# A graph convolution with nearest neighbours: two-piece float32r gathers, a sigmoid adjacency, and thresholds and widening on GpSimd

## What is computed

```python
emb = jnp.einsum('bnc,ec->bne', x_flat, dist_w)          # 32 numbers per point
d2 = sq[:, :, None] + sq[:, None, :] - 2.0 * jnp.einsum('bne,bme->bnm', emb, emb)
dist = jnp.sqrt(jnp.clip(d2, 0.0))
_, idx = jax.lax.top_k(-dist, K)                          # K = 24 nearest
adj = knn_mask & (dist <= THRESHOLD) | eye                # 0/1, 1024 x 1024 per image
X_lin = x_flat @ fc_w.T + fc_b
S = (adj_f / De[:, None, :]) @ adj_f.transpose(0, 2, 1) / Dv[:, :, None]
out_flat = S @ X_lin + x_flat
# batch norm over all images, then o * sigmoid(o)
```

## Time and profile before

| | us |
|---|---|
| median of 3 timed runs | 196.6 |
| lowest, highest | 195.44, 198.93 |
| span of the profiled execution, first to last instruction | 193.5 |
| median less the span (what lies around it) | 3.1 |

### The profile page before, as it was taken

One profiled execution on the slowest core, in us unless ns is written; L12 is line 12 of the kernel. 1 busy time (PEld: TensorE's weight loads), 2 busy tenths in 40 slices (PEclk: granted clock), 3 DMA queues, 4 the chain that ended last, 5 costly groups with the idle time before them and its releaser, 6 DMA issues.

```text
span 193.5 us, 4430 instructions
## 1 busy us (share of the span) xinstructions
PE 167.5 (87%) x1365; PEld 97.3 (50%) x1365; DVE 154.6 (80%) x910; ACT 109.2 (56%) x191; POOL 90.2 (47%) x128
## 2 busy tenths in 40 slices
PE   7888997989799993999999899999989899999300
PEld 2324522664367641755558475555746557947200
DVE  1757999999999298999845799889687987697663
ACT  2047779995769769644446796442476342060291
POOL 1003536489755857932230699964229753600000
PEclk9999999999999999799999999999999999999855
DMA  5801000453257917543430753353342938600038
GB/s 177 314 12 1 2 3 1 75 92 59 55 88 81 28 31 165 81 85 58 56 55 0 59 161 57 59 108 74 41 54 46 159 71 96 126 0 3 0 141 294
DMA packets 44411, 14.85 MB, mean 77 GB/s; under 512 B 41816, under 2 KB 42456, under 8 KB 44384
## 3 DMA queue, kind: packets, MB, share of 16 engines
q1 hardware_dynamic: 43520, 14.14, 40.8%
q10 hardware_dynamic: 864, 0.40, 0.8%
HBM read 4.02 MB, written 2.13 MB: 32 GB/s over the span
## 4 chain that ended last, share of the span: by engine, by line
PE 40%; issue 22%; POOL 20%; ACT 12%; DVE 5%; ACTq 0%; POOLq 0%; DVEq 0%
PE pt L406 10%; PE pg L381 8%; POOL H L713 8%; PE pt L435 5%; PE po L344 4%; PE po L435 3%; POOL tr L688 3%; POOL tp L694 3%; PE pt L456 3%; ACT left L537 3%; PE po L368 3%; PE po L355 2%; ACT key L587 2%; ACT sign L595 2%; DVE xn L1010 2%
## 5 line engine op out<-in xcount | busy, mean ns | idle before, releaser
L809 DVE MAX8 cand<-key 128x8 f32<-128x64 f32 x512 | 82.1, 215 | 0.7
L587 ACT ACTIVATE key<-pg 128x512 f32<-128x512 f32 x64 | 34.5, 592 | 35.4 <-PE pg L381 33.3
L406 PEld LDWEIGHTS pt<-xp,H 128*128 128x128 bf16 x768 | 45.8, 99 | 17.3 <-issue 12.1
L406 PE MATMUL pt<-xp,H 128*128 128x128 bf16 (+1 forms) x768 | 50.7, 223 | 0.0
L381 PE MATMUL pg<-right,left 64*128 64x512 f32 x128 | 40.8, 643 | 6.0 <-ACT key L587 5.2
L595 ACT ACTIVATE sign<-key,thr 128x1024 bf16<-128x1024 f32 x32 | 36.7, 1146 | 11.3 <-DVE thr L835 10.7
L713 POOL TENSOR_SCALAR H<-sign 128x1024 bf16<-128x1024 bf16 x32 | 33.4, 1043 | 2.5
L435 PE MATMUL po<-HT,tp 128*128 128x512 bf16 x144 | 33.8, 380 | 0.0
L708 POOL TENSOR_SCALAR low<-cs 128x1 f32<-128x1 f32 x32 | 6.0, 187 | 55.0 <-ACT sign L595 49.5
L381 PEld LDWEIGHTS pg<-right,left 64*128 64x128 f32 x128 | 12.3, 184 | 15.8 <-ACT key L587 8.3
L435 PEld LDWEIGHTS po<-HT,tp 128*128 128x128 bf16 x144 | 12.9, 98 | 13.7
(11 more groups left out here) (87 smaller groups left out, 181.4 us busy)
## 6 DMA issues: line engine op xcount, KB each, us to landing
out<-xn SPq DMA_DIRECT2D x7, 256.0 KB, 2.2
dvb<-inv_rows SPq DMA_DIRECT2D x3, 512.0 KB, 4.5
x_sb<-x SPq DMA_DIRECT2D x1, 1024.0 KB, 6.0
x_sb<-x SPq DMA_DIRECT2D x1, 512.0 KB, 3.7
HT<-H SPq DMA_TRANSPOSE x32, 3.2
x_sb<-x ACTq DMA_DIRECT2D x1, 256.0 KB, 3.2
x_sb<-x SPq DMA_DIRECT2D x1, 256.0 KB, 3.4
out<-xn SPq DMA_DIRECT2D x2, 128.0 KB, 2.5
```

Of the source, the lines that this page charges most:

```text
L406: mm = pe.matmul(pt[:, j // T_BLOCKS, at:at + wide], lhs, x_cols(b, t, q, wide), start=(t == 0 and j % T_BLOCKS == 0 and q == 0), stop=(t ...
L587: act.activation(key[:, k % KEYS, cols], pg[:, h, :], ACT.Copy).then_inc(s["drained"], 1)
L809: ins = dve.max(cand[:, k % 2, c, :], key[:, k % KEYS, c * CHUNK:(c + 1) * CHUNK])
```

## The change

- The gather's `t32` is split into two float32r pieces in place of three bf16 ones, so a gather is 32 matmuls in place of 48. `t_residual` and `t_middle` go; `t_low` stays on POOL. `tp` has one buffer in place of two.
- The moving operand has to be float32r also: POOL copies each transposed tile from `HT` (now one buffer) to `wide` (`widen`, 128x1024, bf16 to float32r). Tiles 0, 1 of an image are widened in its step 6, tiles 2, 3 in step 7, tiles 4, 5 in step 8 (the next image's step 0), tile 6 in step 10, tile 7 in step 11. Step 31 has tiles 26 to 29, with the wait for their transposes; 30 follows after `mark(31)`; 31 is shared by POOL and ACT.
- ACT writes `H` itself, as a steep Sigmoid with row sum (`adjacency`, now on ACT). POOL no longer writes `H`.
- DVE's threshold instruction goes; POOL forms the bound (`limit`) after the third round, and it is the last thing in POOL's step. POOL's small `mark` stands where `low` stood.
- Flags are summed and read for pairs of tiles (single for the last six); release of a pair is two steps after its second tile. Scatters, gathers, `x` pieces and residuals move to other steps.
- The square roots of the images 2 and 3 and of the batch norm become powers on POOL (`pow`); ACT loads the Sigmoid table after `drain_key(0, 2)` and the Silu table ahead of time, after `spread_copy`.

The core of the diff:

```diff
-X_MIDDLE = {1: (0, 1), 4: (1, 0), 5: (1, 1), 9: (2, 0), 10: (2, 1), 19: (3, 0), 24: (3, 1)}
-X_LOW = {2: (0, 1), 5: (1, 0), 6: (1, 1), 10: (2, 0), 11: (2, 1), 23: (3, 0), 25: (3, 1)}
+X_MIDDLE = {1: (0, 1), 4: (1, 0), 5: (1, 1), 10: (2, 0), 12: (2, 1), 20: (3, 0), 21: (3, 1)}
+X_LOW = {2: (0, 1), 4: (1, 0), 5: (1, 1), 11: (2, 0), 13: (2, 1), 20: (3, 0), 21: (3, 1)}
+WIDEN_STEPS = {6: (0, 1), 7: (2, 3), 8: (4, 5), 10: (6,), 11: (7,)}
...
+        GATHER = {(b, t): (b - 1, n) for b in range(1, B)
+                  for t, n in ((4, 8), (5, 8), (6, 8), (7, 8))[:3 if b == B - 1 else 4]}
+        GATHER.update({(B - 1, 4): (B - 2, 12), (B - 1, 5): (B - 2, 12)})
+        GROUPS = [(a, a + 1) for a in range(0, ALL - 6, 2)] + [(a,) for a in range(ALL - 6, ALL)]
...
+        RELEASE.update({g[1] + 2: [g] for g in GROUPS if len(g) == 2})
+        RELEASE.update({ALL - 4: [(ALL - 6,)], ALL - 3: [(ALL - 5,)], ALL - 2: [(ALL - 4,)],
+                        ALL - 1: [(ALL - 3,), (ALL - 2,)], ALL: [(ALL - 1,)]})
...
+        for a in range(0, ALL - 6, 2):
+            SCATTER[a + 4] += [a]
+            SCATTER[a + 4 if (a + 2) % TILES == 0 else a + 5] += [a + 1]
...
+                if b * TILES + t < ALL:
+                    WIDEN[b * TILES + t] += [b * TILES + i for i in tiles]
+        WIDEN[ALL - 1] += [ALL - 4, ALL - 3]
...
-                    mm = pe.matmul(out_bank(b, part), tp[:, b % 2, q, j * C:(j + 1) * C],
-                                   HT[:, b % 2, j, a:z], start=(j == 0 and q == 0),
+                    mm = pe.matmul(out_bank(b, part), tp[:, q, j * C:(j + 1) * C], wide[:, h, j, a - h * HALF:z - h * HALF],
...
+            scatter(ALL - 3)
             flag(ALL - 1)
             scatter(ALL - 2)
             scatter(ALL - 1)
...
+            def adjacency(k):
...
                 act.wait_ge(s["limited"], k + 1)
...
+                act.activation(H[:, k % HS, :], key[:, k % KEYS, :], ACT.Sigmoid, scale=KEY_SCALE,
+                               bias=bound[:, k % THRS:k % THRS + 1], accum_out=cs[:, b, t:t + 1]).then_inc(s["signed"], 1)
...
-            act.wait_ge(s["stats_done"], 1)
-            act.activation(bn_s[:, 0:1], bn_mv[:, 1:2], ACT.Sqrt, bias=eps_col[:, :]).then_inc(s["bn_sd"], 1)
+            act.activation(warm[:, :], eps_col[:, :], ACT.Silu)
...
+            def widen(k):
+                b, t = divmod(k, TILES)
+                pool.wait_ge(ht_in[t], 16 * (b + 1))
+                if b > 0 and t % TH == 0:
+                    pool.wait_ge(s["o_ready"], 2 * (b - 1) + t // TH + 1)
+                pool.tensor_copy(wide[:, t // TH, :, t % TH * P:(t % TH + 1) * P], HT[:, t, :, :]).then_inc(s["widened"], 1)
...
+            def limit(k):
+                b, t = divmod(k, TILES)
+                pool.wait_ge(s["ranked"], k + 1)
+                if k >= THRS:
+                    pool.wait_ge(s["signed"], k - THRS + 1)
+                pool.tensor_scalar(bound[:, k % THRS:k % THRS + 1], top[:, k % THRS, 2, 7:8], noise[:, b, t:t + 1], -STEEP,
+                                   ALU.min, ALU.mult).then_inc(s["limited"], 1)
+            def mark(k):
                 b, t = divmod(k, TILES)
                 pool.wait_ge(s["signed"], k + 1)
...
-                pool.tensor_scalar(H[:, k % HS, :], sign[:, k % SIGNS, :], -1.0, -0.5, ALU.add, ALU.mult)\
-                    .then_inc(s["clipped"], 1)
+                pool.tensor_scalar(marks[:, k % THRS:k % THRS + 1], cs[:, b, t:t + 1], float(NEAREST), None, ALU.is_le)\
+                    .then_inc(s["marked"], 1)
...
-                        adjacency(k - 1)
+                        mark(k - 1)
                     if k in X_MIDDLE:
                         x_middle(*X_MIDDLE[k])
...
+                    if b > 0 and t == SCALE_STEP + 1:
                         t_low(b - 1)
+                    for kk in WIDEN[k]:
+                        widen(kk)
+                    if b > 1 and t in (5, 6):
+                        residual(b - 2, t - 5)
+                    limit(k)
...
-            for b in range(1, B - 1):
+            for b in range(B - 1):
                 for h in range(2):
                     y_stats(b, h)
```

More of the change, by code:

```diff
@@ L11 @@
 BF16 = mybir.dt.bfloat16
+F32R = mybir.dt.float32r
 I32 = mybir.dt.int32
@@ L384, in flag @@
             def flag(k):
[L385 to L389, removed]
+                pe.wait_ge(s["marked"], k + 1)
+                if k in LEAD and LEAD[k] >= FLAGS:
+                    pe.wait_ge(s["flag_read"], LEAD[k] - FLAGS + 1)
+                g = LEAD[k] if k in LEAD else LEAD[k - 1]
+                pe.matmul(flag_at(g), marks[:, k % THRS:k % THRS + 1], one_b[:, :], start=k in LEAD,
+                          stop=k in TAIL_OF, skip_group_check=True).then_inc(s["flagged"], 1)
             def scatter(k):
@@ L411, in _ @@
             gathered = [0] * B
[L413 to L418, removed]
             def gather(b, n):
                 for i in range(gathered[b], gathered[b] + n):
-                    (part, q), j = gather_order(b)[i // TILES], i % TILES
+                    part, q, j = i // (T_PIECES * TILES), i // TILES % T_PIECES, i % TILES
@@ L481, in _ @@
                     k = b * TILES + t
-                    settled = RELEASE[k - 1] if k > 0 else []
-                    if b > 0 and t == SCALE_STEP[b]:
-                        for kk in settled:
-                            scatter(kk)
                     if k + AHEAD < ALL:
@@ L492, in _ @@
                         flag(k - 1)
-                    if not (b > 0 and t == SCALE_STEP[b]):
-                        for kk in settled:
-                            scatter(kk)
+                    for kk in SCATTER[k]:
+                        scatter(kk)
                     if k in EMB_STEPS:
@@ L621, in _ @@
             drain_key(0, 2)
+            act.activation(warm[:, :], eps_col[:, :], ACT.Sigmoid)
             for h in range(2):
@@ L851, in release @@
-            def release(k):
-                dve.wait_ge(s["flag_read"], k + 1)
-                dve.wait_ge(s["clipped"], k + 1)
-                under = dve.value_load(least_at(k).bitcast(I32))
-                with dve.If(under < UNDER_BITS):
-                    pick(k)
+                    replaced = signal(dve.match_replace(cwork[:, r, 0:CHUNKS * 8], top[:, k % THRS, r, :], src, 2 * FIRST_OUT))
+                    ahead(4 * r + 2, 4 * r + 4)
+                    dve.wait_ge(s["step"], replaced)
@@ new lines, in search, with read_flag, release @@
+                    src = cwork[:, r, 0:CHUNKS * 8]
+                dve.max(top[:, k % THRS, 2, :], cwork[:, 1, :]).then_inc(s["ranked"], 1)
+                ahead(8, 10)
+                for g in RELEASE[k]:
+                    read_flag(g)
+                ahead(10, CHUNKS)
+            def read_flag(g):
+                i = LEAD[g[0]]
+                dve.wait_ge(s["flagged"], g[-1] + 1)
+                dve.tensor_copy(least_at(i), flag_at(i)).then_inc(s["flag_read"], 1)
+            def release(g):
+                i = LEAD[g[0]]
+                dve.wait_ge(s["flag_read"], i + 1)
+                under = dve.value_load(least_at(i).bitcast(I32))
+                with dve.If(under < (UNDER_BITS if len(g) == 2 else UNDER_LAST_BITS)):
+                    for k in g:
+                        pick(k)
@@ L975, in _ @@
                         out_part(b - 2, 1)
-                    if b > 0 and t == SCALE_STEP[b]:
+                    if b > 0 and t == SCALE_STEP:
                         scale_t(b - 1)
-            for k in RELEASE[ALL]:
-                read_flag(k)
-                release(k)
+            for g in RELEASE[ALL]:
+                read_flag(g)
+                release(g)
             invert_dv(B - 1)
-            out_part(B - 2, 1)
+            for h in range(2):
+                out_part(B - 2, h)
             scale_t(B - 1)
             split_last_t(B - 1)
-            for b in range(1, B - 1):
+            for b in range(B - 1):
                 for h in range(2):
```

255 lines of the change are left out of this document (114 added, 141 removed).

## The result

The changed kernel takes 202.83 us (median of 5 runs, 202.35 to 204.43), the kernel before 196.9 beside it; the ratio is 1.033, with a 95% interval of 1.028 to 1.039. So it is slower by 3.3%. The forecast was 196.5 and "within 2%", with 0.25 on slower. Medians here are of all executions of a set; some executions of every kernel fall in a slower state, and the ratios and intervals leave these out.

A forecast was written before the change was run, and what follows sets the result against it. PE's gather matmuls bound the kernel before, POOL's chain with ACT after; `limit(31)` at 164.5 and last scaling at 170.6, plus 12.35, 1.05 and 9.5, made span 193.5, median 196.5; range 188 to 206.

The forecast's parts named there:

- The ring: Loop: POOL's `limit`, ACT's Sigmoid, POOL's `mark` and POOL's other work follow each other and set the pace, 4.45 a step.
- Rival A: Loop: POOL's chain doesn't hold, its work and hand-overs come out a tenth cheaper; 190 on the median, chance 0.30.
- The start: Up to tile 3: its Sigmoid begins at 38.7, where Sign began at 37.69 before; `mark(3)` at 40.0.
- The fixed part of 1.84: Each late POOL step: `limit` 0.20, hand-over 0.05, ACT's Sigmoid 1.33 and `mark` 0.26.
- The works of 65.2: POOL's own work in steps 4 to 31: x pieces, widenings, `t_low`, residuals, noises, one `normalise`; 65.2 us in all.
- rival C: POOL's widenings take 1.22, deciding from about 1.15, and cold scatters cost in full; 203 on the median, chance 0.16.
- The waits of 9.4: Loop, where POOL is held: step 18 4.3, step 9 1.9, small ones 0.8, the rest in steps 28 to 31.
- The last scatters: PE after the last flag: scatters 30 and 31 at 1.5 each, plus 1.0 after idling (ends 0 and 2.5).
- The tail: Last scaling to the end: 12.35 for DVE's chain, 1.05 for power and products, 9.5 from Silu on.
- rival D: ACT: Square outside the Sigmoid's set brings six table loads of 1.28, mostly hidden; 2.6 more, 199, chance 0.03.
- Rival B: PE's gathers: float32r at fp32's pace per pass, 0.54 for 512 columns, deciding from about 0.25; 226, chance 0.09.
- The 3.1 from span to median: Whole kernel: median of the runs taken as 3.1 above the profiled span, so 193.5 became 196.6, put at 196.5.

The follow-up runs named there:

- e1: Changed kernel with `limit(k)` moved from the end of POOL's step to right behind `mark(k-1)`; 193.66 us, ratio 0.989 to the kernel before.
- e8: Changed kernel with 18 unused 512-column matmuls on PE between the scatter of tile 29 and the last flag; 200.83 us, ratio 1.023 to the kernel before.
- e9: Changed kernel with a third, all-zero piece of t in the gathers, 48 matmuls an image in place of 32; 215.26 us, ratio 1.116 to the kernel before.
- e6: Changed kernel with only the four widenings of POOL's step 31 moved behind `mark(31)`; 197.29 us, ratio 1.003 to the kernel before.
- e4: Changed kernel with the widenings of tiles 0 to 25 moved from POOL to ACT, `limit` still last in POOL's step; 208.27 us, ratio 1.061 to the kernel before.
- e12: Changed kernel with `limit` behind `mark`, step 31's widenings behind the last `mark`, POOL's last residuals before its last two widenings; 191.41 us, ratio 0.984 to before.

## Why the prediction was wrong

The mechanism was the one predicted, and the sum was too small. By its own steps, in the profiled execution, which ends 9.1 later than the forecast's span of 193.5:

- **The ring holds the loop: right.** POOL waits for ACT in 30 of 32 steps and ACT for POOL in 22, and e1 takes the ring apart for 9.2. Rival A, that it would not hold, is out.
- **The start: 2.2 late.** The Sigmoid of tile 3 begins at 40.93 where I had 38.7. Of this 1.9 belong to that execution, as said above; the kernel's own start, 39.0 in e8, was forecast well.
- **The fixed part of 1.84: too small.** `limit` takes 0.31, not 0.20 (a group's mean of 309 ns; I had used POOL's small instructions of the earlier trace rows). From `limit` to `mark` it is 52.20 - 50.53 = 1.67, and 0.30 more to the next instruction: 1.97. 28 steps x 0.13 = 3.6 more.
- **The works of 65.2: right within 2,** 63.8 by POOL's timeline. Widenings come 1.01 apart where I took 1.05 (rival C, 1.15 and more, is out); `t_low` is 2.5 for the two and not 2.3.
- **The waits of 9.4: too few, about 13.** Step 18 came as forecast (5.81 - 1.36 = 4.45 against 4.3). Not foreseen in their size were POOL's waits for a gather that still reads `wide`, 2.56 in step 30 and 1.2 in step 16, and for the transpose in step 31, 1.59 against 0.8. From `mark(3)` to `limit(31)` all of it makes 172.51 - 42.25 = 130.3, forecast 124.5: 5.8 more, of which 3.6 are the fixed part, 3.6 the waits, and the works give back 1.4.
- **The last scatters: 1.3 too few.** I added 1.0 for the time after PE's idle stretch, with an upper end of 2.5; it was 2.4 (e8).
- **The tail: right.** 12.35 + 1.05 + 9.5 = 22.9 forecast, 22.7 measured; the power is 0.58 and not 0.25, the last gather 7.75 and not 6.9, both under cover or small. The table load is hidden behind DVE's statistics (the row below), and there are three in all, so rival D is out.
- **Rival B is out:** eighteen float32r matmuls of 512 columns take 4.44, eight 2.13, so 0.23 each. Some 0.2 more comes to each group, which puts eight 0.26 apart (2.06 to the next instruction), past the 0.25 that I had named as B's sign: by its letter the sign is there, and it was set too near. A gather step of PE is 4.7, not 4.5, and far from B's 7.1. The 0.216 was also misread: 10.58 over 48 is 0.220. The rows are the changed kernel's (the load, then a gather group) and e9's:

```profile
184.03 1.28 ACT L662 ACT_TABLE_LOAD   x1
...
91.02 2.13 PE L453 MATMUL po<-wide,tp 128*128 128x512 f32 x8
93.08 1.13 PE L402 MATMUL pg<-right,left 64*128 64x512 f32 x4
```

```profile
164.16 4.44 PE L453 MATMUL po<-wide,tp 128*128 128x512 f32 x18
```

- **The 3.1 from span to median: not a constant.** The profiled execution of the changed kernel took 204.43 with a span of 202.6, 1.8 apart. This hid a part of the miss.

So the step that failed is "about 2.7 lost before the last scaling, about 2.7 gained after it". The gain after it was there (22.7 against 25.6); the loss before it was 5.8 larger in the ring (the fixed part of 1.84, which measured 1.97, and the waits of 9.4, which measured 13) and 1.3 in the scatters (the 1.0, which measured 2.4); the other 2.2 are the start. Where two differences of large sums cancel, a fixed part 7% too small and waits 3.6 too short are enough to turn the result. I gave 0.30 to A, in which POOL's work and the hand-overs come out a tenth cheaper, and to the same a tenth dearer no rival of its own. The 0.25 on slower stood on B and C, and it came about by neither. Of the signs, ACT as what POOL waits for came; `mark` to `mark` is 4.7 in the mean, but the longest are steps 18, 30 and 31, with 7.6 to 8.0, and `limit(31)` comes 7.7 after its third round, not 4 to 6.

I had priced the wait of `widen(29)` in front of `limit(31)`, but had not seen that the last step is an edit by itself: `limit(31)` as the last of POOL's step, behind four widenings that only the last gather needs. e6 moves them for 5.5, which alone makes the change neutral.

## What to carry to other kernels

When a small result passes between two in-order engines once a step, its price is everything that stands between its two instructions in either engine's order, and idle shares don't show it: look for a pair of engines that name each other in the waits (one of the two waits, with the same 49.5, was there before the change too). Put the instruction that another engine waits for first in its step, as soon as its input is there, before moving any work to a third engine; e4 moved 26 us of work off POOL and lost 5, e1 moved one line and won 9. And look at the last round of a loop by itself, since work that was put there for its slack elsewhere has none.

## What was unexpected of the hardware

- DVE's subtractions of two SBUF operands go from 1.30 to 2.5 to 3.5 for two while POOL works in SBUF, and POOL's two casts from 2.03 to 2.49 beside them (e12). The Trainium skill (SBUF — State Buffer, "SBUF: two separate sides") has it that VectorE and GpSimd share one pair of ports as an exclusive lock, taken by a VectorE instruction with two SBUF inputs against a GpSimd instruction that reads SBUF. The runs agree in that both engines are held up; whether it is a lock or a shared rate they do not tell.
- 48 scatter matmuls take 2.94 with PE busy before (e8, at a granted clock of 1.00), and 5.35 after 4.52 idle, at a granted clock of 0.50 (the lower of its two levels, 1.2 and 2.4 GHz).
- A float32r weight load of 128x128 takes 204 ns in the mean, where the gather's bf16 ones are 98 in the trace before; a power of one element a partition on POOL takes 0.58.
